# One second buffer for transposed counts, an earlier swap, x on SyncE's queue, and half a weight turned behind the first count

## What is computed

```python
agg = segment_sum(h[src], dst) / max(deg, 1)
x = x + relu(agg @ W_l.T + b_l + h @ W_r.T)              # L0
h1 = relu(mean(h) @ W1l + b1 + h @ W1r)                  # L1A
x = x + (mean(h1) @ W2l + b2 + h1 @ W2r)                 # L1B
x = x + layernorm(h + relu(h @ W_self.T + b_self + neigh)) * ln_gamma + ln_beta   # L2, by src
x = x + gcn(relu(gcn(h, W1, b1)), W2, b2)                # L3A, L3B
```

## Time and profile before

| | us |
|---|---|
| median of three runs | 657.49 |
| lowest, highest run | 654.67, 658.32 |
| profiled execution | 656.83 |
| its span | 655.0 |
| TensorE busy (share of the span) | 631.1 (96%) |
| VectorE busy | 399.9 (61%) |
| ScalarE busy | 303.4 (46%) |
| GpSimd busy | 85.4 (13%) |

### The profile page before, as it was taken

How to read it: one execution, slowest core, us unless ns; L and a number is a source line. 1 busy time by engine, 2 the same in 40 slices (tenths; PEclk the granted TensorE clock), 3 DMA queues, 4 the chain that set the end, 5 groups by cost and what they waited for, 6 DMA issues and landing times.

```text
span 655.0 us, 11118 instructions
## 1 busy us (share of the span) xinstructions
PE 631.1 (96%) x3047; PEld 511.4 (78%) x3048; DVE 399.9 (61%) x875; ACT 303.4 (46%) x628; POOL 85.4 (13%) x135
## 2 busy tenths in 40 slices
PE   6989999999789999999899999999999999999997
PEld 4547667778668888888688888888888998899886
DVE  6998999967767534453343788754999830441222
ACT  4977776645333445431124241224578753555210
POOL 3442443200000000000000000000354070000000
PEclk9999999999989999999999999999999999999999
DMA  6300325422775520545863266342200000000102
GB/s 222 105 1 2 55 45 80 62 66 75 121 121 155 120 52 7 170 135 134 176 126 48 98 145 174 70 82 57 80 1 1 1 2 1 2 0 1 48 17 95
DMA packets 151843, 48.39 MB, mean 74 GB/s; under 512 B 133500, under 2 KB 137396, under 8 KB 151800
## 3 DMA queue, kind: packets, MB, share of 16 engines
q1 hardware_dynamic: 150520, 45.34, 30.0%
q10 hardware_dynamic: 1280, 2.56, 1.1%
HBM read 30.44 MB, written 17.44 MB: 73 GB/s over the span
## 4 chain that ended last, share of the span: by engine, by line
PE 82%; DMA 5%; DVE 4%; SPq 4%; issue 2%; ACT 1%; DVEq 1%; POOL 0%; ACTq 0%; POOLq 0%
PE ps L1707 30%; PE ps L1800 22%; PE ps L1837 13%; PE ps L1863 8%; PE ps L1686 8%; SPq L478 2%; DMA count_rows<-count_squares 2%; DMA swap<-count 1%; DMA zT<-rows 1%; DVE src_hot L1200 1%; SPq L502 1%; DMA wstage<-in_L_gnn_W_l 1%; PE ps L1700 1%; DVE stats L1172 1%; POOL dst_hot L594 0%
## 5 line engine op out<-in xcount | busy, mean ns | idle before, releaser
L1800 PE MATMUL ps<-p_hi,cstage 128*128 128x512 f32 x400 | 157.2, 393 | 5.6 <-DVE own L1422 4.7
L1800 PE MATMUL ps<-p_lo,cstage 128*128 128x512 f32 x400 | 156.4, 391 | 0.0
L1707 PE MATMUL ps<-w_hi,hT_hi 128*128 128x512 f32 x320 | 126.4, 395 | 2.8 <-DVE hT_lo L1224 2.2
L1707 PE MATMUL ps<-w_hi,hT_lo 128*128 128x512 f32 x320 | 124.7, 390 | 0.0
L1707 PE MATMUL ps<-w_lo,hT_hi 128*128 128x512 f32 x320 | 124.6, 389 | 0.0
L1800 PEld LDWEIGHTS ps<-p_hi,cstage 128*128 128x128 f32 x400 | 75.6, 189 | 23.4 <-DVE own L1422 5.8
L1800 PEld LDWEIGHTS ps<-p_lo,cstage 128*128 128x128 f32 x400 | 75.7, 189 | 15.6
L1686 PE MATMUL ps<-src_hot,dst_hot 128*128 128x320 bf16 x420 | 67.4, 306 | 5.8 <-DVE src_hot L1200 2.7
L1707 PEld LDWEIGHTS ps<-w_hi,hT_hi 128*128 128x128 f32 x320 | 60.1, 188 | 16.2 <-issue 3.6
L1200 DVE TENSOR_SCALAR src_hot<-iota,nodeT 128x640 bf16<-128x640 f16 x210 | 68.3, 381 | 6.1 <-PE ps L1686 4.0
L1707 PEld LDWEIGHTS ps<-w_hi,hT_lo 128*128 128x128 f32 x320 | 60.1, 188 | 12.6
(11 more groups left out here) (156 smaller groups left out, 965.5 us busy)
## 6 DMA issues: line engine op xcount, KB each, us to landing
rows<-squares SPq DMA_DIRECT2D x38, 256.0 KB, 2.5
zT<-rows SPq DMA_DIRECT2D x120, 64.0 KB, 2.5
count_rows<-count_squares SPq DMA_DIRECT2D x10, 320.0 KB, 2.2
countT<-count_rows SPq DMA_DIRECT2D x40, 80.0 KB, 3.2
x<-in_x ACTq DMA_DIRECT2D x1, 2304.0 KB
out_x<-x SPq DMA_DIRECT2D x9, 256.0 KB
wstage<-rows SPq DMA_DIRECT2D x32, 64.0 KB, 2.5
wstage<-in_L_gnn_W SPq DMA_DIRECT2D x2, 1024.0 KB, 5.5
```

The source lines that it names most:

```text
L1707: last = nc.tensor.matmul(ps[:, bank, :], a[:, r, k, :], w[:, slot, k, :], start=n == 0, stop=n == len(pairs) - 1)
L1800: last = nc.tensor.matmul(ps[:, AGG + r, :], cstage[:, part, k, :], p_[:, k, :], start=n == 1, stop=n == 2 * len(parts) * NT)
```

## The change

Counts are squared into three places: buffer 0 for blocks 0 to 4 (BY_COUNTING = 5), and two more, used in turn, for blocks 5 to 9; the second of these lies in the part of vec that zT takes later. A transpose waits for the parking of the one before in its own buffer. In the counting loop block b's merged end now squares block b - 4, not b - 2, so that none is squared at b = 2 and 3 and one at b = 8. Counts 5 and 6 are squared in the tail between counting and aggregation, 7 to 9 behind the combinations of tiles 0 to 2. VectorE's split of the weight in L0's aggregation moves from i == 4 to i == 5 (ScalarE's stays). SyncE issues x behind the first weight's halves. The swap's step is cut in two, "so" (out) behind park 3 of L1B and "si" (in) behind park 7; it stood behind park 9. TensorE turns the third and fourth chunk of L0's first weight behind the first count and not ahead of it.

```diff
-                     enumerate((p_lo_at + 8 * D * 4, relued_at))]
+                     enumerate((p_lo_at + 8 * D * 4, relued_at, vec_at + 3 * D * 4))]
-    BY_COUNTING = 6
+    BY_COUNTING = 5
+    def count_buffer(b):
+
+        return 0 if b < BY_COUNTING else 1 + (b - BY_COUNTING) % 2
+
+    def wait_counts_parked(engine, b):
+
+        uses = b + 1 if b < BY_COUNTING else (b - BY_COUNTING) // 2 + 1
+        engine.wait_ge(counts_parked[count_buffer(b)], 16 * uses)
...
-            order = [("f", 0), ("f", 1), ("f", 2), ("v", rows[0]), ("v", rows[1])]
+            order = [("f", 0), ("f", 1), ("x", None), ("f", 2), ("v", rows[0]), ("v", rows[1])]
...
-            order += [("tp", 6)] + loads[1:2] + [("tr", 6), ("tp", 7), ("tr", 7), ("tp", 8)] + parks(L1A, 0)
-            order += [("tr", 8), ("tp", 9)] + parks(L1A, 1) + [("tr", 9)] + turns(L1A, 0, 1) + [("v", rows[2])]
+            order += [("tp", 5), ("tp", 6), ("tr", 5), ("tr", 6)] + loads[1:2] + [("tp", 7), ("tr", 7), ("tp", 8), ("tr", 8)]
+            order += [("tp", 9)] + parks(L1A, 0) + [("tr", 9)] + parks(L1A, 1) + turns(L1A, 0, 1) + [("v", rows[2])]
...
-            order += loads[3:4] + parks(L1B, 0, 1) + turns(L1B, 0, 1) + [("v", rows[6])] + parks(L1B, 2, 3, 4, 5)
-            order += loads[4:5] + turns(L1B, 2) + parks(L1B, 6) + turns(L1B, 3) + parks(L1B, 7, 8, 9) + [("s", None)]
+            order += loads[3:4] + parks(L1B, 0, 1) + turns(L1B, 0, 1) + [("v", rows[6])] + parks(L1B, 2, 3) + [("so", None)]
+            order += parks(L1B, 4, 5)
+            order += loads[4:5] + turns(L1B, 2) + parks(L1B, 6) + turns(L1B, 3) + parks(L1B, 7) + [("si", None)]
+            order += parks(L1B, 8, 9)
...
+                elif kind == "x":
+
+                    sp.wait_ge(first_loaded[1], 16)
+                    sp.wait_ge(x_pad_set, 1)
+                    dma_rows(sp, x_dram, x, x_loaded)
...
-            act.wait_ge(first_loaded[1], 16)
-            act.wait_ge(x_pad_set, 1)
-            dma_rows(act, x_dram, x, x_loaded)
...
-            act.sem_inc(counts_parked, 16)
...
-                if b - 2 < BY_COUNTING:
-                    square_counts(b - 2)
+                if b > 3:
+                    square_counts(b - 4)
...
+            square_counts(BY_COUNTING)
             dve.wait_ge(top_turned, 1)
...
             p_rest(L0, NT - 1, 1)
+            square_counts(BY_COUNTING + 1)
             first_own(NT - 1)
...
-                        if i == 4 + late:
+                        if i == (5 if s == L0 else 4 + late):
                             split_weights(s + 1, 1)
                         combine(i, i % 2)
-                        if s == L0 and i < NT - BY_COUNTING:
-                            square_counts(BY_COUNTING + i)
+                        if s == L0 and i + 2 < NT - BY_COUNTING:
+                            square_counts(BY_COUNTING + 2 + i)
...
-            turn_first(0, (2, 3))
-
             visited = [pe.alloc_register(f"pe_visited{h}") for h in range(2)]
...
             count(0, 0, visits_of(pe, visited, 0, 0))
+            turn_first(0, (2, 3))
             turn_first(1, (0, 1))
```

More of the change, by code:

```diff
@@ L251, in gnn_kernel @@
     parked, turned_in, weight_in = [[sem(f"{what}{r}") for r in range(2)] for what in ("parked", "turned_in", "weight_in")]
-    counts_squared, counts_parked = sem("counts_squared"), sem("counts_parked")
+    counts_squared, counts_parked = sem("counts_squared"), [sem(f"counts_parked{k}") for k in range(3)]
     hidden_done, u_pads, biased, span_coarse, span_exact = (
@@ L470, in _ @@
                     sp.wait_ge(counts_squared, what + 1)
-                    sp.dma_start(count_rows[what], count_squares[what >= BY_COUNTING][:, :]).then_inc(counts_parked, 16)
+                    sp.dma_start(count_rows[what], count_squares[count_buffer(what)][:, :]
+                                 ).then_inc(counts_parked[count_buffer(what)], 16)
                 elif kind == "tr":
-                    sp.wait_ge(counts_parked, 16 * (what + 2))
+                    wait_counts_parked(sp, what)
                     if what > 1:
@@ L504, in _ @@
                                          (turned_in if s is not None else weight_in)[r], 16)
-                elif kind == "s":
+                elif kind == "so":
                     sp.wait_ge(counts_squared, NT)
-                    sp.wait_ge(counts_parked, 16 * (NT + 1))
-                    parts = [(WIN * q, NS * (1 - q)) for q in range(2)]
                     for k, (a, f) in enumerate(parts):
                         sp.dma_start(swap[k], count16[a:a + WIN, :, f:f + NS]).then_inc(swap_out, 16)
+                elif kind == "si":
                     sp.wait_ge(swap_out, 32)
@@ L1239, in square_counts @@
             def square_counts(b):
-                k = int(b >= BY_COUNTING)
-                if k:
-                    dve.wait_ge(counts_out, NW + 2)
-                else:
-                    dve.wait_ge(counts_out, 2 * b + 4)
-                dve.wait_ge(counts_parked, 16 * (b + 1))
+                k = count_buffer(b)
+                dve.wait_ge(counts_out, 2 * b + 4 if b < BY_COUNTING else NW + 2)
+                if 0 < b < BY_COUNTING:
+                    wait_counts_parked(dve, b - 1)
+                elif b > BY_COUNTING + 1:
+                    wait_counts_parked(dve, b - 2)
                 nc.vector.transpose(count_squares[k][:, :], count16[:, b, :]
@@ L1348, in _ @@
             dve.wait_ge(deg_done, 5)
-            dve.wait_ge(counts_parked, 16 * (BY_COUNTING + 1))
+            wait_counts_parked(dve, BY_COUNTING - 1)
             p_rest(L0, NT - 2, 0)
```

1 line of the change is left out of this document (added).

## The result

The changed kernel takes **648.42 us** (median of 4 runs, 647.29 to 649.95), the kernel before 657.89 beside it (4 runs). The ratio is 0.987, 95% interval 0.983 to 0.991: faster by 1.3%. 647.5 was forecast, with a range of 643.8 to 651.5. The profiled execution took 648.9 with a span of 647.1, which is 7.9 less than the span of before; 9.6 were forecast.

What follows compares the result with a forecast made beforehand. TensorE works 96% of the span, so only its waits and slow stretches can give time. 6.3 + 2.3 + 2.2 − 1.2 = 9.6 us off the 655.0 span gives 645.4; with run overhead 647.5 us, range 643.8 to 651.5.

Steps and rivals of the forecast that it cites:

- zT asked for near 180: Sign in L0's aggregation: zT's first reads issued near 180 us, against 186.51 before; wrong if after 184.
- no wait at tile 4 of L1B: Sign in the third convolution's products: no wait at its fifth tile, where TensorE idled 2.2 us for hT_lo.
- no granted clock under 1 in the first aggregation: Sign in L0's aggregation: the slow clock behind the long wait, about 1.7 us, goes.
- the wait at its ninth tile: Sign in L0's aggregation: one wait of 1 to 2 us, for cstage or own behind zT.
- The loop: Counting loop: no square ahead of the next count in blocks 2 and 3, 1.15 us each, 2.3 us gained.
- The swap: L1B's products: swap issued earlier, so tile 4's turned reads come in time; 2.2 us gained, bounds 1.5 to 2.2.
- Counts 5 and 6 early: Ahead of L0's aggregation: both squares fit VectorE's idle times and cost nothing; one step of SyncE's chain of four goes.
- L0's aggregation: First convolution: waits and slow clock, 8.3 us, go, less 2.0 left; 6.3 us gained, bounds 3 to 8.3.
- The rival in which SyncE's chain stays late: L0's aggregation: reads of 5, 6 and W1r hold count 7's landing 3 us; 3 gained, not 6.3; 650.8 us; chance 0.12.
- The second buffer: L0's aggregation: counts 8 and 9 no longer wait for a buffer; part of the 6.3 us gain.
- The start: Up to the loop: head gains 0.2, the half weight turned later costs 1.4; net loss 1.2 us.
- The rival of the falling clock: First count: TensorE idles 3 us ahead, then runs at 1.2 GHz; 1.7 us more, 649.2 us; chance 0.08.

Runs made afterwards that it cites:

- loop_back: control with the squares of counts 0 to 4 two blocks later in the counting loop again (block b squares b − 2); 650.07 us.
- swap_back: control with both halves of the swap behind the last park of L1B again; 651.72 us.
- late_first_tiles: control with hT_hi and hT_lo of L1A's first two tiles one tile later in L0's aggregation; 644.96 us, ratio 0.979.
- one_buffer: control with counts 5 to 9 all squared into one place, each waiting for the park before; 649.61 us.
- all_three_one_buffer: all_three with a single place for counts 5 to 9 in place of two; 646.85 us.
- all_three: control with half_back's and late_first_tiles' edits, and W2l's load with two bias rows behind the turned reads of tile 3; 642.15 us, ratio 0.975.
- dummy_turns: control with eight more transposes ahead of the first count, their results overwritten; 648.57 us.
- half_back: control with the third and fourth chunk of the first weight turned ahead of the first count again, x still on SyncE; 647.20 us.
- control: changed kernel with the table of windows stored as uint16, not int32, as in all experiments; 649.13 us, ratio 0.985.
- start_filled: start_as_before with eight more transposes ahead of the first count, into a bank that the count clears; 648.25 us, ratio 0.984.
- start_as_before: half_back with x issued by ScalarE, so the start of the kernel before; 649.75 us.
- w1r_early: control with the load of W1r between the turned reads of counts 5 and 6, not behind both; 648.88 us.

## Why the prediction was right, and where it was not

The time was forecast within 1 us, and part of that is luck. The aggregation gave 2.5 us less than forecast; the start lost 0.7 less and L1B gained 0.4 more, which took back nearly half of it. Of the signs that the prediction named, zT asked for near 180, no wait at tile 4 of L1B, the counts of 3.3 us and the second count near 30 came true; no granted clock under 1 in the first aggregation did not, and the wait at its ninth tile was 2.4 and not 1 to 2.

**The loop** (2.3 forecast, 2.17 measured, 2.18 by loop_back): right in mechanism and size. The counts of blocks 2 and 3 now take 3.26 us.

**The swap** (2.2 forecast, 2.59 measured, 2.5 by swap_back): right in mechanism. The bound of 2.2 was too low, since I took the wait alone: before, the 144 matmuls behind it took 33.04 us, where 240 without a wait take 54.40, which makes 32.64. The other 0.4 lies in the matmuls behind the wait.

**Counts 5 and 6 early.** That VectorE's two squares ahead of the aggregation would be hidden held for VectorE: they start at 142.41 and 145.54. Between the two stands the reduction that leads to ScalarE's first stage, at 144.41 and still waiting 0.50 for TensorE. From L0's last products to the aggregation TensorE took 0.24 longer all the same, with a wait of 0.34 for cstage that the kernel before did not have. No run separates that.

**L0's aggregation** (6.3 forecast, 3.81 measured) is the step that failed, in two places. First, the sum took 6.7 us for every step of SyncE's queue, "the first a little less or more, since W1r lies ahead of it". The first took 8.5, since the park flew 4.9 us under W1r's bytes, where 3.4 was the longest such row I had. zT landed 36.8 us after the start of the aggregation, not 35.6, and TensorE waited 2.4 and not 1.4. Second, the forecast let TensorE restart at full pace behind that wait. In the profile after it ran at 0.50 for 3 us, and the last 40 matmuls took 10.93 us, against 9.56 where the clock stayed up behind such a wait (loop_back, swap_back): 1.4 us. I had priced a slow clock only behind the 4 us wait of the earlier trace rows and given a remaining wait of 1.4 none. Together with the 1.0 this is 2.4 of the 2.5 that were missed. The second term is not in every execution: two of the four runs after have a mean granted clock of 1.000 and spans of 645.5 and 646.2, the other two one of 0.997 and 647.1 and 648.2. late_first_tiles shows both terms to hang on one cause, the place of zT's instructions ahead of tile 8's stage, and gives 4 us back at once.

The rival in which SyncE's chain stays late names that very mechanism (reads of 5 and 6 and W1r hold the landing of count 7), with 3 us as its size. It holds with 1.2 us, and its time, 650.8, was too high.

**The second buffer.** The prediction put "counts 8 and 9 no longer wait for a buffer" among the causes of the 6.3. VectorE's wait is gone, but one_buffer says that this by itself moved 0.7; all_three_one_buffer says that it is worth 4.4 when nothing else holds tile 8. L0's aggregation in the four cases, in us (the right column has the other edits of all_three as well):

| | zT ahead of the stage | zT one tile later |
|---|---|---|
| one place for counts 5 to 9 | 50.38 | 50.02 |
| two places | 49.65 | 45.58 |

So the buffer is neither idle nor the cause of the gain here: from one place and zT ahead, taking away either wait alone gives 0.7 or 0.4, and both give 4.8.

**The start** (a loss of 1.2 forecast, 0.46 measured): right in mechanism, too high in size. The first count begins 0.34 earlier (13.22 against 13.56) and is 0.09 shorter, where 0.2 was forecast. From its end to the first product it is 21.92 us against 21.03: turning the half behind the count cost 0.89, where 1.4 was forecast. dummy_turns against half_back, 46.72 against 45.52, gives 1.20 for it with TensorE at pace in the first count on both sides. The rival of the falling clock said that fewer transposes might slow the first count. In the profiled executions that count was slow already in the kernel before (12.87 us, and 20 matmuls in 14 to 18, as in the control), so nothing was lost there. Why it was slow before is open: the pause ahead of it was 1.38 us, as long as in half_back, where it took 11.6. With x on SyncE and the half ahead the first product came at 45.5 in half_back and all_three, and at 48.0 in all_three_one_buffer.

The Trainium skill (TensorE: Matmul & The Clock Gate, The HAM clock gate) says that the number of matmuls spent at the lower level at a kernel's start varies from run to run of the same kernel. The traces fit that: with 16 transposes or more ahead of the count four profiled executions (half_back, all_three, dummy_turns, start_filled) went through it in 11.6 us and three (before, start_as_before, all_three_one_buffer) in 12.7 to 12.9, and all_three and all_three_one_buffer differ in nothing up to there. With eight transposes none of seven reached 11.6 (12.8 to 13.8). So with transposes ahead the count can be fast but need not be, as far as one profiled execution of each kernel tells. The Trainium skill (TensorE: Matmul & The Clock Gate, PE-mode transpose) says that the full clock does not engage for transposes. start_filled speaks against that here: of its 24 transposes ahead of the count the first eight take 1.97 us, the next 1.79 and the last 1.04, with nothing else on TensorE between them but the two of 20x20 for the table (0.22).

## What to carry to other kernels

Where two waits stand one behind the other, taking away one can show little (0.7 and 0.4 here, 4.8 for both); take both away before calling a buffer useless. When a wait for data is left, look what the waiting engine has queued behind it that does not need the data: moving that ahead was worth 4 us here, though zT was asked for 1.9 later than in the control. Before reading a difference between two runs as the edit's, compare the stages that the edit does not touch: loop_back and swap_back had a clock that did not fall, two runs had a row of 3.03 us on GpSimd, and these are worth 1.4 and 1.0 us, more than some of the edits. And idle slots ahead of a stage that TensorE paces are a place to try its work in, even work that could stand elsewhere.

## What the hardware showed that was not expected

**The granted clock column can read 1.00 while TensorE runs at the lower level.** At 8 us eight transposes take 1.97 us in every trace, behind the first count 1.04 to 1.17. In the ten traces with a slow first count 17 to 22 matmuls run in 14 to 18 us, in the other four 26 or 27; nine of the ten have a column of 1.00 there, only start_as_before shows 0.64. At the start the pitch of the matmuls tells, not the column.

**A wait of 2.2 to 2.6 us may or may not be followed by the lower level.** Behind 2.2 (control), 2.4 (after), 2.5 (dummy_turns, start_filled), 2.7 (w1r_early), 3.2 (half_back) and 3.9 us (start_as_before) the last two tiles took 10.92 to 10.96; behind 2.5 (loop_back) and 2.6 (swap_back) 9.56 and 9.57, with the granted clock at 1.00 throughout. Executions of one kernel differ too: the control's four runs have a mean granted clock of 0.996, 0.997, 1.000 and 0.997, and the one at 1.000 is the fastest, 647.42 against 649.09 to 650.00. The kernels without that wait, late_first_tiles and all_three, stay at 0.999 to 1.000 in all eight runs.

**A transfer pays for what was issued ahead of it on its queue.** Parks of 320 KB land after 2.9 to 3.5 us behind four turned reads, and after 4.5 to 6.6 us behind eight and a load of 1 MB (4.9 after, where the load went out 2.4 us earlier; 6.6 in one_buffer, where it was 1.6); a park of 256 KB behind a load of 1 MB took 8.1 in late_first_tiles.

**One row of GpSimd's can take 0.6 to 3.03 us.** Its one-hot rows (128x128, L612) mostly take 0.6 to 1.0 us, and 1.57 in some places, such as that of the earlier trace rows. In start_filled and all_three_one_buffer one of them, begun at 29.52 and at 30.57 in the middle of VectorE's one-hot rows, took 3.03 and ended at 32.55 and 33.60, each 0.15 after VectorE's row at which that series broke off (32.40 and 33.45). No run tests whether VectorE is the cause.
